# Filling the score stacks of a gated cross-attention straight from SBUF, with queries and keys in one buffer

## The reference

```python
def xattn(x, c, Wq, bq, Wk, bk, Wv, bv, Wo, bo):      # per batch
    q, k, v = Wq @ x + bq, Wk @ c + bk, Wv @ c + bv     # [128, 512]
    q, k, v = (split into 8 heads of 16 channels, [512, 16] each)
    q, k = rope(q, 8), rope(k, 8)      # rotates the first 8 channels of a head, passes the other 8
    p = softmax(q @ k.T / sqrt(16))    # 512 x 512 per head
    return Wo @ concat(p @ v) + bo

x = x + tanh(g_xattn) * xattn(layernorm(x), ctx, ...)
h = silu(layernorm(x) @ gate.T) * (layernorm(x) @ up.T)        # weights in FP4, 1408 wide
x = x + tanh(g_ffn) * rmsnorm(h @ down.T)
```

## Time and profile before

| | |
|---|---|
| median of 3 runs | 924.72 us (924.64 to 926.47) |
| the profiled execution | 918.37 us, span of its instructions 916.6 us |
| PE busy / PEld | 815.8 us (89%) / 421.6 us |
| DVE / ACT / POOL busy | 522.1 / 483.6 / 178.5 us |
| mean granted clock of TensorE | 0.945 |
| DMA | 86.44 MB |

### The profile page before, as it was taken

How to read it: one execution, slowest core, us unless ns; L and a number is a source line. 1 busy time by engine, 2 the same in 40 slices (tenths; PEclk the granted TensorE clock), 3 DMA queues, 4 the chain that set the end, 5 groups by cost and what they waited for, 6 DMA issues and landing times. The chain is left out here.

```text
span 916.6 us, 13653 instructions
## 1 busy us (share of the span) xinstructions
PE 815.8 (89%) x5110; PEld 421.6 (46%) x5142; DVE 522.1 (57%) x760; ACT 483.6 (53%) x895; POOL 178.5 (19%) x174
## 2 busy tenths in 40 slices
PE   3378999999998988999993599999999999999997
PEld 1123333333333333334332376666666666666664
DVE  4398977888987867888871961314131423141113
ACT  2227776887787766778792552325231623252223
POOL 1232333333333423331112820000000000000000
PEclk8559999999999988999996889999999999999999
DMA  5678555666665666465212010002000110000001
GB/s 167 171 198 218 155 142 153 189 200 194 170 165 152 175 175 189 119 167 153 69 33 79 8 46 1 1 1 67 25 1 1 47 45 0 0 27 21 0 1 46
DMA packets 55176, 86.44 MB, mean 94 GB/s; under 512 B 19274, under 2 KB 20938, under 8 KB 55114
## 3 DMA queue, kind: packets, MB, share of 16 engines
q1 hardware_dynamic: 55114, 85.62, 33.0%
HBM read 44.70 MB, written 34.34 MB: 86 GB/s over the span
## 5 line engine op out<-in xcount | busy, mean ns | idle before, releaser
L670 DVE TENSOR_REDUCE neg_max<-s_ps 128x2 f32<-128x1024 f32 x256 | 310.0, 1219 | 61.8 <-PE s_ps L420 60.8
L536 ACT ACTIVATE probs<-st_ps 128x512 f32<-128x512 f32 x512 | 277.9, 597 | 105.5 <-PE st_ps L432 101.2
L448 PE MATMUL pv_ps<-probs,v_ones 128*32 128x256 f32 x2048 | 166.1, 397 | 12.6 <-ACT pv_sb L542 12.6
L1098 PE MATMUL gu_ps<-x_head,gu_head 128*128 128x512 f32 x352 | 155.9, 443 | 0.0
L965 DVE TENSOR_TENSOR hidden<-gu_ps,silu 128x512 f32<-128x512 f32 x44 | 30.4, 691 | 202.6 <-ACT silu L1040 202.6
L420 PE MATMUL s_ps<-k_stack,q_stack 48*128 48x512 f32 x512 | 135.4, 526 | 10.5 <-DVE neg_max L670 8.4
L1099 PE MATMUL gu_ps<-x_rest,gu_head 128*128 128x512 f32 x352 | 139.0, 395 | 0.0
L1040 ACT ACTIVATE silu<-gu_ps 128x512 f32<-128x512 f32 x44 | 26.3, 597 | 204.8 <-PE gu_ps L1101 204.8
L432 PE MATMUL st_ps<-q_stack,k_stack 50*128 50x512 f32 x512 | 110.6, 421 | 12.9 <-DMA q_stack<-max_scratch 12.7
L420 PEld LDWEIGHTS s_ps<-k_stack,q_stack 48*128 48x128 f32 x512 | 50.4, 193 | 121.1 <-issue 81.1
L1115 PE MATMUL y_ps<-dn_head,h_head 128*128 128x512 f32 x176 | 101.5, 577 | 1.1 <-DVE h_rest L967 1.0
(11 more groups left out here) (114 smaller groups left out, 807.1 us busy)
## 6 DMA issues: line engine op xcount, KB each, us to landing
q_stack<-image SPq DMA_DIRECT2D x64, 192.0 KB, 3.9
k_stack<-image SPq DMA_DIRECT2D x64, 192.0 KB, 4.5
image<-split_head SPq DMA_DIRECT2D x32, 256.0 KB
image<-split_head SPq DMA_DIRECT2D x64, 128.0 KB
image<-split_rest SPq DMA_DIRECT2D x32, 256.0 KB
ct<-ctx_dram SPq DMA_DIRECT2D x16, 256.0 KB, 5.5
swap<-proj SPq DMA_DIRECT2D x64, 64.0 KB, 2.0
scale_of<-inverse_scratch SPq DMA_DIRECT2D x16, 256.0 KB
```

The costliest lines, as they stand in the source:

```text
L448: last = nc.tensor.matmul(pv_ps[2 * KC * j:2 * KC * (j + 1), cols], v_ones[b % 2][:, kt, j, quad, :], probs[at % PROBS][:, j, cols], start ...
L536: nc.scalar.activation(probs[at % PROBS][:, tile % 4, :], st_ps[item % ST_BANKS][:], ACT.Exp).then_inc(st_read, 1)
L670: nc.vector.tensor_reduce(neg_max[j // 2][:, :, j % 2, qt], s_ps[item % S_BANKS][:], AXIS_X, ALU.max, negate=True).then_inc(s_read, 1)
L1098: nc.tensor.matmul(gu_ps[t % 2][:, half], head, x_head[:, k], start=(k == 0), stop=False)
```

## The change

The way over `image` is dropped. All 128 output channels of q are projected in one full-width matmul and all of k in another, with an order of channels such that the eight rotated and the eight passed channels of a head lie in one block of partitions. cos is 1 and sin 0 in the passed rows, so the rotation runs over whole tiles of q and k side by side (1024 columns). Rounding and difference are one instruction each (`split`, four planes of 512 columns). Six transfers then fill the stack of a batch: for each of the three 16-row blocks and each of the two halves one, that reads 64 partitions of `split` and writes 16 partitions of the stack, 16 KB in each. Queries and keys share one buffer (`stacks`), and there are three of them. Each fill moves 256 KB, 1.5 MB a batch. The projections move to slots 9 and 12, the value projection to slot 5, the rounding to slot 4; `merge_quads` is one transfer (was four), `store_inverse` one (was two), `load_inverse` two (was one).

```diff
-X_TILES, C_TILES, PROBS = 8, 4, 3
-MIX_AT, ROT_AT, PASS_AT, V_AT = 1, 2, 5, 8
+X_TILES, C_TILES, PROBS, STACKS = 8, 4, 3, 3
+MIX_AT, HEADS_AT, V_AT, Q_AT, K_AT = 1, 4, 5, 9, 12
+Q_REST, Q_HEAD, K_HEAD, K_REST = range(4)
+BLOCKS = ((Q_HEAD, K_HEAD), (Q_HEAD, K_REST), (Q_REST, K_HEAD))
...
+            def fill_stacks(sp, n, blocks):
+                stack = stacks[n % STACKS]
+                for at in blocks:
+                    q, k = BLOCKS[at]
                     for odd in two:
+                        rows = stack[STACK * odd + KC * at:STACK * odd + KC * (at + 1)].bitcast(F32)
+                        pair = split[STACK * odd:STACK * (odd + 1), q:k + 1:k - q, :].bitcast(F32)
+                        sp.dma_start(rows.rearrange("c j w t -> c (j w t)"), pair).then_inc(stack_in[n % STACKS], 16)
+
+            def build_stacks(sp, n):
+                if n >= STACKS:
+                    sp.wait_ge(st_full, last_weight(n - STACKS, 1))
+                sp.wait_ge(heads, n + 1)
+                fill_stacks(sp, n, (0,))
+                sp.wait_ge(rests, n + 1)
+                fill_stacks(sp, n, (1, 2))
...
             def sync_step(sp, b):
-                nxt, proj_n = b + 1 < B, b + AHEAD_PROJ
-                if nxt:
-                    load_half(sp, b + 1, 1)
+                nxt = b + 1 < B
                 store_max(sp, b, 1)
-                if proj_n < B:
-                    swap_partners(sp, proj_n)
                 if b:
                     gather_sums(sp, b - 1, 1)
+                load_max(sp, b, 1)
+                if b:
                     merge_quads(sp, b - 1)
-                load_max(sp, b, 1)
-                if b >= 2:
-                    store_x(sp, b - 2)
-                if b:
                     store_inverse(sp, b - 1)
-                if proj_n < B:
-                    store_head(sp, proj_n, 1)
                 if b + 2 < B:
-                    load_half(sp, b + 2, 0)
+                    build_stacks(sp, b + 2)
                 if nxt:
                     store_max(sp, b + 1, 0)
                 if b:
                     load_inverse(sp, b - 1)
-                if proj_n < B:
-                    store_rest(sp, proj_n, 1)
-                if b + 5 < B:
-                    load_inputs(sp, b + 5)
+                if b + 4 < B:
+                    load_inputs(sp, b + 4)
                 if nxt:
                     load_max(sp, b + 1, 0)
+                if b >= 2:
+                    store_x(sp, b - 2)
                 gather_sums(sp, b, 0)
-                if proj_n < B:
-                    store_head(sp, proj_n, 0)
-                    store_rest(sp, proj_n, 0)
+                if b + AHEAD_PROJ < B:
+                    swap_partners(sp, b + AHEAD_PROJ)
...
+            def by_cosine(engine, ops, n):
+                engine.wait_ge(st_read, ST_NO["k", n] + 1)
+                ops.tensor_tensor(turned[:], proj[:], both(cos), ALU.mult).then_inc(cosine, 1)
+
+            def by_sine(engine, ops, n):
+                engine.wait_ge(swapped, SWAPS * (n + 1))
+                ops.tensor_tensor(swap[:], swap[:], both(sin), ALU.mult).then_inc(sine, 1)
                 engine.wait_ge(cosine, n + 1)
                 engine.wait_ge(sine, n + 1)
+                ops.tensor_tensor(proj[:], swap[:], turned[:], ALU.add).then_inc(rotated, 1)
+
+            def split_rests(engine, ops, n):
+                engine.wait_ge(heads, n + 1)
+                ops.tensor_tensor(split[:, Q_REST:K_REST + 1:K_REST - Q_REST, :], proj[:],
+                                  split[:, Q_HEAD:K_HEAD + 1, :].bitcast(F32), ALU.subtract).then_inc(rests, 1)
...
             def pool_step(pool, b):
+                if b + 2 < B:
+                    by_sine(pool, nc.gpsimd, b + 2)
+                if b + AHEAD_PROJ < B:
+                    normalise(pool, nc.gpsimd, b + AHEAD_PROJ)
+                if b + 2 < B:
+                    split_rests(pool, nc.gpsimd, b + 2)
                 if b >= 2:
                     residual(pool, nc.gpsimd, b - 2)
...
                 if b:
                     scale_heads(pool, nc.gpsimd, b - 1)
+                if b + AHEAD_PROJ < B:
+                    by_cosine(pool, nc.gpsimd, b + AHEAD_PROJ)
```

More of the change, by code:

```diff
@@ L68, in transposed_items @@
     for n in range(AHEAD_PROJ):
[L69 removed]
+        items += [("q", n), ("k", n)]
     for b in range(B):
@@ L74, in transposed_items @@
                 items.append(("mix", b - 2))
[L75 to L78, removed]
+            if slot == Q_AT and b + AHEAD_PROJ < B:
+                items.append(("q", b + AHEAD_PROJ))
+            if slot == K_AT and b + AHEAD_PROJ < B:
+                items.append(("k", b + AHEAD_PROJ))
     items += [("mix", B - 2), ("mix", B - 1)]
@@ L120, in attend @@
         proj = sb("proj", [P, 2, T], F32)
[L121 to L127, removed]
+        swap, turned = sb("swap", [P, 2, T], F32), sb("turned", [P, 2, T], F32)
+        split = sb("split", [P, 4, T], F32R)
+        stacks = [sb(f"stacks{n}", [P, PAIRS, 2, T], F32R) for n in range(STACKS)]
+        v_ones = [sb(f"v_ones{p}", [P, KT, QUAD, V_WIDTH], F32) for p in two]
         probs = [sb(f"probs{n}", [P, QUAD, T], F32) for n in range(PROBS)]
@@ L175, in attend @@
         rotated = sem("rotated")
[L176 to L181, removed]
+        heads = sem("heads1")
+        rests = sem("rests1")
+        stack_in = [sem(f"stack_in{n}") for n in range(STACKS)]
         max_head = [sem(f"max_head{h}") for h in two]
@@ L185, in attend @@
         max_out = [sem(f"max_out{h}") for h in two]
-        max_in = [[sem(f"max_in{p}{h}") for h in two] for p in two]
+        max_in = [[sem(f"max_in{n}{h}") for h in two] for n in range(STACKS)]
         pv_done = sem("pv_done")
@@ L216, in swap_partners @@
             def swap_partners(sp, n):
-                sp.wait_ge(st_read, ST_NO["rot", n] + 1)
+                sp.wait_ge(st_read, ST_NO["k", n] + 1)
                 if n:
[L219 to L230, removed]
@@ L419, in score @@
                     rows = slice(STACK * odd, STACK * odd + DATA_ROWS)
-                    last = nc.tensor.matmul(out[:, odd, :], q_stack[p][rows, j, qt * P:(qt + 1) * P], k_stack[p][rows, j, :],
+                    last = nc.tensor.matmul(out[:, odd, :], stacks[p][rows, j, 0, qt * P:(qt + 1) * P], stacks[p][rows, j, 1, :],
                                             start=True, stop=True)
@@ L480, in _ @@
                 pe.wait_ge(weights_in, WEIGHTS)
-                project_rot(pe, 0)
-                project_pass(pe, 0)
+                for which in "qk":
+                    project(pe, 0, which)
                 pe.wait_ge(const_in, CONSTS)
@@ L485, in _ @@
                 for n in (1, 2):
-                    project_rot(pe, n)
-                    project_pass(pe, n)
+                    for which in "qk":
+                        project(pe, n, which)
                 pe.wait_ge(scales_f32, 2)
```

277 lines of the change are left out of this document (99 added, 178 removed).

## The result

The changed kernel took 1050.15 us (median of 4 runs, 1046.08 to 1056.17); the kernel before took 925.60 us beside it (924.64 to 931.17). The ratio is 1.134 (95% interval 1.126 to 1.142): 13% slower. Forecast were 1013 us and a range of 886 to 1040, so the direction was right and the time lies outside the range: 37 us above the forecast, 10 above the range's upper end.

A forecast was written before the change was run, and what follows sets the result against it. Bound: DVE's floor plus the maxima's way over SP. Thirteen steps +84, start +2, batch 14's clock drop +2.6, tail -0.5: +88 on 918.4 gives 1006.5, as a median 1013 us; range 886 to 1040.

The forecast's parts named there:

- The bound: Attention is a chain of steps at DVE's floor, plus the maxima's way over SP wherever that is longer than the step.
- the place: In SP's queue, the fills stand ahead of the store of the maxima.
- hidden beside DVE's 25: POOL's work in a step, some 13.5 us of 25 and about 4 us more than before, was taken to cost nothing.
- The fills' term: Six transfers into 16 partitions, rate extrapolated by partition count to 124 GB/s: 12.7 us of fills a batch.
- my chain: Maxima's way from the first weigh: reciprocal 13.0, issues 14.2, fills 26.9, store landed 28.3, load landed 30.85 us.
- clock term: PE's wait of 5.4 us in every step drops the clock, costing 2.6 us ahead of slot 6: 33.45 us a step.
- 13.0 + 2.6: Reciprocal of slot 6 done 13.0 us after the first weigh, plus 2.6 us lost to the clock drop.
- the load of the maxima: On SP's queue behind the maxima's store: 0.55 us of issue and 2.0 to land, at the end of each step's chain.
- the tail: After attention, the merge and the inverse store lose issues: -0.5 us.
- one sign: Sign of being right: the load of the maxima is PE's longest wait in every step, near 5 us.
- Rival 1: Fills no slower than transfers of 48 partitions (231 GB/s, 6.8 us), waits go: median 892 us, range 884 to 905; chance 0.26.
- Rivals 2 and 3: 2: even, fills at 165 to 180 GB/s, 920 to 930, chance 0.03. 3: 77 GB/s, about 1108, chance 0.04.

The follow-up runs named there:

- the kernel with early fills: At 2.1 us a step: interleaved rows, inputs late, fills before the inverse's store, 936.42 us. At 47.4 and 38.6 us: changed kernel, only fills moved so, 1031.88 us.
- the kernel with late inputs: The changed kernel with a step's two input tiles issued behind the load of the maxima instead of ahead of it; 1019.17 us.
- the kernel with two blocks: The changed kernel with only two of the three blocks filled, four transfers instead of six; 979.14 us.
- the kernel with 128 partitions: The changed kernel with the same bytes in six transfers over 128 partitions, into a tile that nothing reads; 919.19 us.
- the kernel with spread rows: The changed kernel with its six transfers into every fourth partition of a tile that nothing reads, instead of 16 lying together; 946.88 us.

## Why the prediction was right and where it failed

*The bound was right, and so was the place, but for a second one (below).* The way of the maxima over SP decides, the fills ahead of their store are what lengthens it, the load lands last ([4.49 <-DMA stacks<-max_scratch] at 283.47), and the clock falls behind each wait. In this kernel the engines' own work cost nothing, as forecast; rounding takes 0.68 us instead of 0.84. Where the waits for DMA are gone, "hidden beside DVE's 25" is wrong for POOL's wide instructions: they hold up DVE, by 2.1 us a step in the kernel with early fills.

*The fills' term held nearly.* I took 124 GB/s and 12.7 us. The window above has 121 over 14 us, which is more than the fills' bytes; in the kernel with late inputs the windows within the fills have a little less, by which the fills take 13.5 to 14.4 us:

```profile
284.00:287.00 3.00, 2.49 (x21) 1.14 (x18) 2.40 (x3) 2.49 (x6) 0.00 (x0) 1.00 1.04 109
287.00:290.00 3.00, 3.00 (x26) 0.96 (x24) 1.91 (x3) 2.43 (x5) 0.00 (x0) 1.00 1.09 116
```

The load was issued 31.3 us after the first weigh; my chain with its clock term has 28.3 + 2.6 = 30.9. The reciprocal came 0.7 earlier than my 13.0 + 2.6. From it to the landing of the fills (278.19) it was 16.4 us where 1.2 + 12.7 stood, 2.5 more, and the store landed with them instead of 1.4 later. The estimate of 14.4 us from the Trainium skill (SBUF — State Buffer, section "Door 1: The DMA port swizzle (why `[64,N]` ≈ `[32,N]`)") was the nearer for the fills. But the extrapolation was right for a wrong reason: I scaled by the number of partitions, and 16 partitions spread out run at 241 GB/s.

*The step that failed is the load of the maxima:* "2.0 to land, the figure of a small transfer", with "The inverse and the inputs (0.8 MB at 404 GB/s, 2 us) pass while the store lands". They don't pass. They are issued by 269.6, behind all fills and the store in the queue, so their packets come when the fills end, which is just when the load is issued. It took 5.3 us where 2.55 stood, 2.75 more in a step; that is 2.75 of the 3.16 us by which the step shown above is longer than 33.45. With the inputs out of the way it took 3.1, with the inverse too 1.9. This is the mis-sized term.

The sum by parts, against the profiled execution of 1056.17 us and my 1006.5, is 49.7 us. Batch 0 weighs at 68.72 instead of 64: 4.7. Batch 2 weighs at 137.45, where 90 + 33.45 = 123.45 stood: 9.3 more behind batch 0. From there to batch 14 (574.03) twelve steps take 36.38 us instead of 33.45: 35.2. The rest, 0.5, is the tail. (The median stands 6.0 us below this execution, where I had put it 6.3 above; so the medians differ by 37 and not by 50.) What SP's queue held around batch 2's fills:

```profile
66.63 0.60 SPq L249 DMA_DIRECT2D stacks<-max_scratch  x2
67.27 1.14 SPq L333 DMA_DIRECT2D packed<-gate_up_packed_dram  x2
68.44 1.52 SPq L335 DMA_DIRECT2D packed<-down_packed_dram  x1
...
77.20 5.24 SPq L230 DMA_DIRECT2D stacks<-split  x6
...
93.07 0.56 SPq L249 DMA_DIRECT2D stacks<-max_scratch  x2
```

The fills of batch 2 went out at 77.20, where I had 73. Ahead of them stand the feed-forward weights (1.08 MB) that I had left out; what share of the 9.3 us is theirs was not tried.

*Half of one sign was missed.* I looked for one wait a step. PE first needs the stack of the batch after next in `score`, at the head of the next step, and waits there too (61.4 us). By the total it was the larger of the two (52.2 for the maxima), but in the kernel with early fills it fell by 47.4 us while the wait for the maxima rose by 38.6: both have to be shortened together, as in the kernel with two blocks (4.4 and 38.4 us). My list called a wait for `stacks<-split` a wrong place; it was a second place on the same chain.

*The rivals.* Rival 1 (231 GB/s, 892 us) was right in its mechanism: with the fills at 382 GB/s the changed kernel takes 919, with them at 241 it takes 947. It promised too much: the kernel with 128 partitions has no wait of PE for stacks or maxima left and still a step of 27.6 us, not 25.4, with DVE held up for 22.9 us. Rivals 2 and 3 did not occur. (Rival 3's 1108 is also some 5 us less than its own terms give: 13 times 7.7 us on top of 1013.) The clock term (2.6 us a drop) held in the forecast's steps: the reciprocal ended 14.9 us after the first weigh where 13.0 + 2.6 stood. A drop costs more where it lasts, as in the slots of 2.16 us above.

*The range* ended at 1040 because its own upper end, 105 GB/s, moved only the fills. No bound was put on the landing of the load (2.75 us in each of 13 steps) nor on the start (14.0 of the 49.7 us are lost by batch 2's first weigh), and these took it out of the range.

## What to carry to other kernels

Count a transfer by where its rows lie in SBUF, not by its bytes: 29% fewer bytes took 19% more DMA time, and one stride in a slice gave half of the loss back. A small transfer on the critical path costs what stands before it at the DMA engines when it is issued, from any queue; list these packets and ask whether they have left by then, not whether they were issued long ago. When a load is moved ahead of others, price whoever waits for those. When the waits are gone, look at how long the small instructions of the bounding engine last beside another engine's wide ones, not only at who waits for whom.

## What the hardware showed

- 16 partitions that lie together took 109 to 121 GB/s, 16 in every fourth of 64 took 241, 16 in every third of 48 took 186, 48 together 174 (share 0.87, with 7.71 us of issuing), and 128 took 382, all from the same tile. The Trainium skill (SBUF — State Buffer, section "Door 1: The DMA port swizzle (why `[64,N]` ≈ `[32,N]`)") has partitions 0 to 15 reach four ports, and its table of ports puts 16 spread over 0 to 63 on eight, and partitions 32 to 47 on the same four as 0 to 15. An estimate by that table: rows 0 to 47 put two thirds of their bytes on four ports, so they run at one and a half times the rate of 16 together, 164 to 182 GB/s. The trace is near it with 174 and 186. For eight ports the Trainium skill's page has 189 to 218; here it was 241.
- Transfers from DRAM into 48 partitions ran at 231 GB/s at a share of 1.03, those from SBUF at 174 at 0.87 and, interleaved, at 186 at 1.04. Why is open; I ran nothing that separates the source from the size of the packets there.
- Two halves of SBUF written from two queues: 118 GB/s, no more than one. The Trainium skill (SBUF — State Buffer, section "Can I just issue two DMAs to hit both halves?") has 6% more for two transfers on the two halves; the trace agrees that it brings next to nothing.
- A load of 8 KB landed 1.9 us after its issue with nothing ahead, 3.1 behind 0.26 MB, 5.3 behind 0.79 MB, and 10.8 when issued from ACT's queue while SP's fills ran.
- A DVE cast and a DVE subtraction of 128x16, 0.17 us each, lasted up to 2.3 us when they began while a POOL instruction of 128x1024 was under way, and ended with it; reductions out of PSUM did not. In the kernel with spread rows the granted clock fell to 0.50 behind the waits of PE that this led to, and a slot took 2.16 us instead of 1.23.
